# Position attention: the negated maxima become rows 96 to 98 of the query stack, moved there by DMA

## The reference

```
s[i, j]  = sum over 8 channels of q[i, .] * k[j, .]        i, j in 0..255   (k from ctx, q from x)
e[i, j]  = exp((s[i, j] - max over keys of s) * 8 ** -0.5)
o        = gamma * (v . e) / (sum of e) + x,   then layer norm over the 256 features
```

## Time and profile before

| | |
|---|---|
| median of 3 runs | 5330.28 us (5327.88 to 5330.65) |
| the profiled execution, its time | 5329.21 us |
| its span, first to last instruction | 5327.4 us |
| mean granted TensorE clock | 0.964 |
| PE, DVE, ACT, POOL busy | 88%, 63%, 40%, 30% of the span |

### The profile page before, as it was taken

How to read it: one execution, slowest core, us unless ns; L and a number is a source line. 1 busy time by engine, 2 the same in 40 slices (tenths; PEclk the granted TensorE clock), 3 DMA queues, 4 the chain that set the end, 5 groups by cost and what they waited for, 6 DMA issues and landing times.

```text
span 5327.4 us, 87975 instructions
## 1 busy us (share of the span) xinstructions
PE 4706.2 (88%) x32773; PEld 3287.9 (62%) x32773; DVE 3372.7 (63%) x6404; ACT 2108.9 (40%) x4198; POOL 1580.3 (30%) x3212
## 2 busy tenths in 40 slices
PE   8988985999979889883799999999987999999788
PEld 6766884666646677772466666666664556565455
DVE  5665245777767577787555555555545666666698
ACT  4543122545434333331344444444443343434222
POOL 1111015333312233432333333333332222222122
PEclk9999997999989999995899999999998999999899
DMA  1021002333310000001100000000001000000000
GB/s 41 2 61 46 1 6 62 73 76 76 74 48 1 5 8 8 8 7 65 44 1 1 1 1 1 1 1 1 1 1 36 5 6 5 5 6 4 3 15 16
DMA packets 106071, 109.35 MB, mean 21 GB/s; under 512 B 12144, under 2 KB 98353, under 8 KB 101169
## 3 DMA queue, kind: packets, MB, share of 16 engines
q1 hardware_dynamic: 105648, 103.72, 7.5%
HBM read 86.90 MB, written 16.78 MB: 19 GB/s over the span
## 4 chain that ended last, share of the span: by engine, by line
PE 47%; DVE 19%; issue 15%; POOL 10%; ACT 4%; DMA 3%; SPq 1%; POOLq 0%; DVEq 0%; ACTq 0%
PE banks L2207 12%; PE banks L2358 4%; POOL factors L2718 4%; PE banks L727 3%; PE banks L2343 2%; DMA stack<-parts_x 2%; PE banks L1172 2%; PE banks L2216 2%; PE banks L1761 2%; PE banks L754 2%; DVE neg_max L1085 1%; DVE stats L257 1%; PE banks L2226 1%; PE banks L1671 1%; PE banks L499 1%
## 5 line engine op out<-in xcount | busy, mean ns | idle before, releaser
L263 POOL TENSOR_TENSOR var_eps<-mean_var,ln_eps 128x1 f32<-128x1 f32 x384 | 83.6, 218 | 1633.3 <-DVE mean_var L259 1088.8
L1085 DVE TENSOR_REDUCE neg_max<-banks 128x2 f32<-128x512 f32 x512 | 343.6, 682 | 184.6 <-PE banks L1075 178.1
L1202 ACT ACTIVATE exps<-banks 128x512 f32<-128x512 f32 x512 | 304.8, 597 | 305.8 <-PE banks L1156 288.7
L2252 DVE TENSOR_REDUCE square_sums<-squares 128x4 f32<-128x512 f32 x256 | 174.7, 682 | 257.5 <-ACT squares L2244 253.5
L246 ACT COPY xT<-banks 128x256 f32<-128x256 f32 x160 | 59.7, 373 | 622.5 <-PE banks L238 359.2
L2265 POOL TENSOR_TENSOR factors<-mean_squares,minus_half 128x4 f32<-128x4 f32 x256 | 258.6, 1010 | 21.4
L2207 PE MATMUL banks<-wq,xT 128*128 128x512 f32 x512 | 245.8, 603 | 14.9 <-ACT xT L246 14.9
L1761 PEld LDWEIGHTS banks<-yT,w_swiglu 128*128 128x128 f32 x2048 | 238.2, 193 | 30.2 <-issue 30.0
L1075 PE MATMUL banks<-stack,stack 128*128 128x256 bf16 x1024 | 202.4, 281 | 60.7 <-DMA stack<-parts_x 55.2
L1761 PE MATMUL banks<-yT,w_swiglu 128*128 128x128 f32 x2048 | 247.4, 277 | 8.6 <-DVE hidden L1785 8.6
L2694 ACT ACTIVATE squares<-q_normed 128x512 f32<-128x512 f32 x160 | 100.8, 630 | 387.4 <-DVE q_normed L2684 387.4
(11 more groups left out here) (379 smaller groups left out, 11938.5 us busy)
## 6 DMA issues: line engine op xcount, KB each, us to landing
contextT<-in_ctxT SPq DMA_DIRECT2D x96, 128.0 KB, 3.1
parts_context<-parts SPq DMA_DIRECT2D x96, 64.0 KB, 2.0
parts_x<-parts SPq DMA_DIRECT2D x96, 64.0 KB, 2.0
stack<-parts_context SPq DMA_DIRECT2D x32, 192.0 KB
stack<-parts_x SPq DMA_DIRECT2D x32, 192.0 KB
x_all<-in_x SPq DMA_DIRECT2D x1, 4096.0 KB, 14.2
context<-in_ctx SPq DMA_DIRECT2D x64, 64.0 KB, 2.2
context<-in_ctx SPq DMA_DIRECT2D x32, 128.0 KB, 2.3
```

The lines of the kernel that those rows point to most:

```text
L1085: v.tensor_reduce(self.mx[s][:, :, g:g + 1], self.bM[g % 2].rearrange("p (h c) -> p h c", h=DH), AX.X, ALU.max, negate=True).then_inc(self ...
L1202: self.nc.scalar.activation(self.e[n % 8][:], self.bE[n % 2].rearrange("p (l c) -> p l c", l=DH), ACT.Exp, scale=self.TOK ** -0.5).then_in ...
```

## The change

- The scores no longer add the maxima with matmuls through `select` (L1156 and its table go). Instead SP moves the three rows of bf16 parts out of `neg_maxT` by three DMAs (`move_max_sp`) into rows 96, 97 and 98 of the query stack, and rows 96 to 127 of the key stack hold 1.0, set once by four more memsets on POOL. The score matmul then runs over all 128 rows, the maximum matmul over rows 0 to 95.
- `move_max_sp` stands first in SP's step, with lag 4, ahead of `stack_sp` with lag 2. The first score of a tile waits for the moves.
- The maxima are reduced two heads at a time (128 x 1024 from two banks, 8 instructions, odd ticks). The transposed maxima take one turn in the rotation of the two score banks, so the head scored next but one waits until ACT has copied them.
- Scores start at tick 10, not 6; a group is weighed in two halves two ticks apart; the last half of a tile stands at tick 13 of step t + 5, and `out_dve` and `tail_pool` run in step t + 6, the reciprocal in two halves.

```diff
-    STEP, SCORES_FROM = 16, 6
+    STEP, SCORES_FROM, TURN_AT = 16, 10, 4
+    ROWS, MAX_ROWS = 96, 128
+    TURN_SLOT = STEP - SCORES_FROM + TURN_AT
...
     def setup_pool(self, pool):
         for i in (0, 1):
             for n in range(self.STACK_BUFFERS):
-                pool.memset(self.kq[i][n][:].bitcast(I32), 0)
+                last = pool.memset(self.kq[i][n][:].bitcast(I32), 0)
+        last.then_inc(self.zeroed.sem, 1)
+        pool.wait_ge(self.zeroed.sem, self.zeroed.at(1))
+        for n in range(self.STACK_BUFFERS):
+            last = pool.memset(self.kq[0][n][self.ROWS:self.MAX_ROWS], 1.0)
+        last.then_inc(self.zeroed.sem, 1)
...
-            v.tensor_reduce(self.mx[s][:, :, g:g + 1], self.bM[g % 2].rearrange("p (h c) -> p h c", h=DH), AX.X, ALU.max, negate=True).then_inc(self.maxed.sem, 1)
+            v.tensor_reduce(self.mx[s][:, :, 2 * i:2 * i + 2].rearrange("p h g -> p g h"), self.bM[i % 2].rearrange("p g (h c) -> p g h c", h=DH),
+                            AX.X, ALU.max, negate=True).then_inc(self.maxed.sem, 1)
...
+    def slot_free(self, eng, slot):
+
+        t, n = divmod(slot - 2, self.HEADS + 1)
+        if slot < 2 or (n == self.TURN_SLOT and t + 1 >= self.NT):
+            return
+        if n == self.TURN_SLOT:
+            eng.wait_ge(self.m_copied.sem, self.m_copied.all(Tile(t + 1)))
+        else:
+            eng.wait_ge(self.exped.sem, self.exped.at(Tile(t), n + 1 - (1 if n > self.TURN_SLOT else 0)))
...
+    def move_max_sp(self, sp, t, s):
+
+        sp.wait_ge(self.m_copied.sem, self.m_copied.all(t))
+        for j in range(3):
+            sp.dma_start(self.stack(1, t)[self.ROWS + j:self.ROWS + j + 1, :, :],
+                         self.mT[s][32 * j:32 * j + self.HEADS, :]).then_inc(self.m_moved.sem(t), 16)
...
         for l in range(DH):
-            out = self.bE[n % 2][:, l * D:(l + 1) * D]
-            self.nc.tensor.matmul(out, k[:, h, l * P:(l + 1) * P], q[:, h, :], start=True, stop=False)
-            last = self.nc.tensor.matmul(out, self.sel[:, h, :], self.mT[s][:], start=False, stop=True)
+            last = self.nc.tensor.matmul(self.bE[self.slot(t, n) % 2][:, l * D:(l + 1) * D], k[rows, h, l * P:(l + 1) * P], q[rows, h, :], start=True, stop=True)
...
-            "pe": [[(5, self.score_late_pe), (4, self.score_pe), (4, self.turn_max_pe), (3, self.max_pe)]],
+            "pe": [[(6, self.weigh_last_pe), (5, self.score_late_pe), (4, self.score_from_pe), (4, self.turn_max_pe), (3, self.max_pe)]],
             "act": [[(5, self.exp_late_act), (4, self.exp_act), (4, self.copy_max_act)]],
-            "dve": [[(4, self.split_max_dve), (5, self.out_dve), (3, self.max_dve)]],
-            "pool": [(3, self.values_pool), (5, self.tail_pool), (1, self.split_pool)],
-            "sp": [(2, self.stack_sp), (1, self.parts_sp), (0, self.source_sp)],
+            "dve": [[(4, self.split_max_dve), (6, self.out_dve), (3, self.max_dve)]],
+            "pool": [(3, self.values_pool), (6, self.tail_pool), (1, self.split_pool)],
+            "sp": [(4, self.move_max_sp), (2, self.stack_sp), (1, self.parts_sp), (0, self.source_sp)],
```

More of the change, by code:

```diff
@@ L1117, in copy_max_act @@
     def copy_max_act(self, act, t, s):
-        for _ in range(4):
+        for _ in range(self.TURN_AT):
             yield
@@ L1121, in copy_max_act @@
         if begun(t - 2):
[L1122 to L1123 removed]
+            act.wait_ge(self.m_moved.sem(t - 2), self.m_moved.all(t - 2))
+        self.nc.scalar.copy(self.mT[s][:], self.bE[self.turn_slot(t) % 2].bitcast(BF16)[:, 0:D]).then_inc(self.m_copied.sem, 1)
+    def move_max_sp(self, sp, t, s):
[3 more added lines that the diff above has]
+                         self.mT[s][32 * j:32 * j + self.HEADS, :]).then_inc(self.m_moved.sem(t), 16)
     def values_pool(self, pool, t, s):
@@ L1165, in weigh @@
                 pe.wait_ge(self.o_read.sem, self.o_read.all(t - 2))
-        for part in range(4):
-            l, ones = divmod(part, 2)
+        for ones in (0, 1):
             for g in range(4):
@@ L1171, in weigh, with weigh_at, score_from_pe, score_late_pe @@
                 out = self.bO[s][32 * g:32 * g + 32, ones * D:(ones + 1) * D]
-                last = self.nc.tensor.matmul(out, left, self.e[n % 8][:, l, :], start=(r == 0 and part == 0),
+                last = self.nc.tensor.matmul(out, left, self.e[n % 8][:, l, :], start=(r == 0 and l == 0 and ones == 0),
                                              stop=(r == 3 and l == DH - 1), skip_group_check=True)
-        last.then_inc(self.weighed.sem, 1)
-    def score_pe(self, pe, t, s):
-        for tick in range(self.STEP):
-            if tick >= self.SCORES_FROM:
+        if l == DH - 1:
+            last.then_inc(self.weighed.sem, 1)
+    def weigh_at(self, pe, t, s, tick):
+        r, after = divmod(tick - self.SCORES_FROM - 5, 4)
+        if 0 <= r < 4 and after % 2 == 0:
+            self.weigh(pe, t, s, r, after // 2)
+    def score_pe(self, pe, t, s):
+        for tick in range(self.SCORES_FROM, self.STEP):
+            self.score(pe, t, s, tick - self.SCORES_FROM)
+            self.weigh_at(pe, t, s, tick)
+            yield
+    def score_from_pe(self, pe, t, s):
+        for _ in range(self.SCORES_FROM):
+            yield
+        yield from self.score_pe(pe, t, s)
+    def score_late_pe(self, pe, t, s):
+        for tick in range(self.STEP, 2 * self.STEP):
+            if tick - self.SCORES_FROM < self.HEADS:
                 self.score(pe, t, s, tick - self.SCORES_FROM)
-            for r in range(4):
-                if tick == self.SCORES_FROM + 4 * r + 5:
-                    self.weigh(pe, t, s, r)
+            self.weigh_at(pe, t, s, tick)
             yield
[L1185 to L1192, removed]
+    def weigh_last_pe(self, pe, t, s):
+        for tick in range(2 * self.STEP, 2 * self.STEP + 2):
+            self.weigh_at(pe, t, s, tick)
             yield
@@ L1218, in out_dve @@
         v = self.nc.vector
-        for _ in range(9):
+        yield
+        yield
+        dve.wait_ge(self.weighed.sem, self.weighed.all(t))
+        for half in (0, 1):
+            at = slice(half * P, (half + 1) * P)
+            v.reciprocal(self.rd[:, at], self.bO[s][:, D + half * P:D + (half + 1) * P]).then_inc(self.o_read.sem, 1)
             yield
-        dve.wait_ge(self.weighed.sem, self.weighed.all(t))
-        v.reciprocal(self.rd[:], self.bO[s][:, D:2 * D]).then_inc(self.o_read.sem, 1)
+            yield
+        dve.wait_ge(self.o_read.sem, self.o_read.at(t, 2))
+        v.scalar_tensor_tensor(self.on[s][:], self.bO[s][:, 0:D], self.gamma[:, 0:1], self.rd[:], ALU.mult, ALU.mult).then_inc(self.o_read.sem, 1)
         yield
-        dve.wait_ge(self.o_read.sem, self.o_read.at(t, 1))
-        v.scalar_tensor_tensor(self.on[s][:], self.bO[s][:, 0:D], self.gamma[:, 0:1], self.rd[:], ALU.mult, ALU.mult).then_inc(self.o_read.sem, 1)
         yield
```

63 lines of the change are left out of this document (36 added, 27 removed).

## The result

| | before | after |
|---|---|---|
| median | 5330.20 us (5327.88 to 5330.65, 4 runs) | 5407.51 us (5405.15 to 5419.81, 4 runs) |
| the profiled execution, its time and span | 5329.21, 5327.4 us | 5406.08, 5404.3 us |
| mean granted TensorE clock | 0.964 | 0.951 |
| PE, DVE, ACT, POOL busy | 88%, 63%, 40%, 30% | 86%, 62%, 39%, 29% |

The kernel became slower: 1.0151 times before, 95% interval 1.0133 to 1.0168. The forecast was 5399 us, in a range of 5338 to 5435.

What follows compares the result with a forecast made beforehand. Before, PE's work and a two-step loop through `mean_var`, POOL and the stack were taken to be in balance. Memsets 14.0, fill 2.0, 29 x (21.35 - 19.35) and drain -4.6 gave 69.4 us more: 5399 us, range 5338 to 5435.

Steps and rivals of the forecast that it cites:

- Loop of one step: From a PE step's first maximum matmul (S) through copy, moves and stack to PE's next start: 19.8 us.
- The falls: PE's idle lowers the clock in nine of ten steps, 1.7 us each: mean step 21.35 us.
- rival 1: The clock holds in PE's idles, so the step is 19.8 us and the kernel 5352 us; chance 0.22.
- 96 rows cost what 128 do: Maximum matmuls over 96 rows save PE nothing; at three quarters, 0.9 us of work would go.
- What I left off the path: Parts, DVE's work (some 15 us a step) and the moves' landing (0.9 us to spare) don't limit the step.
- two-step way: Through POOL, `mean_var` and the splits: parts land at S + 24.7 us, before SP comes to the stack at S + 26.9.
- Memsets: Four more memsets of ones on POOL, ahead of the first stack: 14.0 us by elements, 7.0 by bytes.
- Fill: Step 4, the first with a move ahead of a stack: 18.8 us in place of 16.8, +2.0.
- Drain: From tile 31's first maximum matmul to the last output's end: 44.0 us in place of 48.6, -4.6.
- The forecast's own range: 5360 to 5412 us, with moves at 1.2 to 1.95 us, memsets at 7 or 14, seven to ten falls in ten steps.
- Rival 2: The stack lands 2.5 us sooner, PE bounds a step of 16.6 us, the kernel takes 5259 us; chance 0.10.

Runs made afterwards that it cites:

- e4: The changed kernel with 22 matmuls of 256 columns that nobody reads ahead of each of PE's waits for a stack: 5357.80 us.
- e11: The changed kernel with POOL's splits first, the ones set by DVE, and the stack ahead of the moves on SP: 5265.47 us.
- e5: The changed kernel with the transpose of the maxima one tick earlier: 5384.36 us.
- e8: The changed kernel without the three moves and SP's wait for the copy, the maxima left out of the scores: 5345.73 us.
- e6: The changed kernel with the ones set by DVE beside POOL's zeros: 5389.69 us.
- e2: The changed kernel with the key stack's repeated blocks loaded one by one, nine DMAs in place of six: 5334.89 us.
- e7: The changed kernel with the key stack loaded by blocks, the transpose one tick earlier and the ones set by DVE: 5329.48 us.
- e1: The changed kernel with the moves issued by ACT behind its copy, the stack first on SP: 5431.82 us.

## Why the prediction was right

Each term as forecast, and what the traces show.

- **Loop of one step.** Forecast S to copy 5.1, wait and moves 1.95, stack to PE 12.77: 19.8 us. Measured in the chain above 5.05, 1.93 (1235.83 to 1237.76) and 12.78: 19.76. Taking the price of the moves from three stores in pieces of 512 B, not from stack loads, was right: SP needs 1.81 us for them.
- **The falls.** Forecast 0.9 x 1.7 us a step. The copy ended 6.4 to 8.0 us behind S in 25 of the 29 steps and 5.04 in four. Step 21.57 against 21.35, and e4 puts the falls at 1.67 us a step on average (48.4 us in all; forecast 44). That is fewer falls than forecast, but dearer ones: 48.4 over 25 is 1.94 us each, not 1.7. In 15 of them the copy came 1.3 to 1.6 us late, in the other ten 2.0 to 2.9. The Trainium skill's account ("TensorE: Matmul & The Clock Gate", section "HAM oscillation": a wait for a transfer in each tile throttles each tile) agrees in kind with these 25 of 29, though the waits of its example (about 3 to 5 us) are longer than most of those here. The prediction put the price of all 29 falling at 3 us over its sum; by its own terms it is 29 x 0.1 x 1.7 = 4.9.
- **But the argument for them was weaker than its result.** I expected idles of 3.6 us, beyond the 3.2 of the earlier trace rows, with PE's work at 16.2 us. e11 shows PE's work to be 16.99 us with nothing to wait for: 0.8 more. A half group takes 1.00 us in the chain above and the pair behind it 0.33 in place of 0.22, so 1.11 in all where I had 1.02, eight times a step. So the idles are about 2.6 us (2.2 to 3.8), near the 2.5 after which the clock held in the earlier trace rows. By that row I should have given rival 1 more than 0.22. The clock fell all the same, after 2.6 us here and after an idle of 1.8 us in e5 (at 1136.0 us), while it held after 2.8 us in the rows above and after 3.0 us at tile 6 (1036.5 us). That the falls came as forecast is thus in part luck: the length of idle they were argued from was not there, and no row of before shows an idle between 2.5 and 3.2 us.
- **96 rows cost what 128 do.** In the chain a pair of L1191 (128 rows) and a pair of L1088 (96 rows) take 0.22 us each.
- **What I left off the path.** Parts on the two-step way: forecast S + 24.7 us, in e8 1174.04 to 1198.93, 24.9. DVE: 158.7 us over 11.3 steps of e11, 14.0 a step, below PE's 17. The moves land before the first score: PE waited for them once in the section, 0.4 us.
- **Memsets.** Forecast 14.0, by elements: 13.87 for the four on POOL. On DVE (e6) each is recorded with 3.47 us too, but they start 4.27 us apart, with 0.80 us between them.
- **Fill.** Forecast +2.0 for the first step with a move: 929.99 to 948.81 us, 18.82 in place of 16.78. Tile 2 stands 15.25 us later than in the earlier trace rows, with the section beginning 0.7 us sooner.
- **Drain.** Forecast -4.6, measured 46.9 against 48.6 us: -1.7. Mis-sized by the same error in PE's half groups, in part; in e11, at full clock, it is 45.4 (1431.03 to 1476.47), where I had 42.3. The other 2 us were not taken apart.
- **Sum.** 15.25 + 29 x 2.22 - 1.7 = 78 us, against 76.9 between the profiled executions and 69.4 forecast. The forecast was 8 us low: 6.4 us in the step (0.22 x 29) and 2.9 in the drain, less 0.75 in the fill.
- **The forecast's own range.** 5360 to 5412 was not added up rightly at its upper end: with the loop at 19.8, ten falls in ten and memsets at 14, the terms give 16.0 + 29 x 2.15 - 4.6 = 74 us, 5403 us. The 5407.5 us measured are beyond that, since a fall cost 1.94 us and the drain gave 1.7 in place of 4.6.

Rival 2 (faster, 5259 us) was right in one thing: a step of about 17 us, PE bound, was to be had. The way to it is the order on SP and POOL, not a landing shortened by chance. Its counter-argument held in part: by the Trainium skill's "DMA: Bandwidth & Descriptors", section "Why a DMA increments its semaphore by 16 and not by 1", a repeated block of three runs on three engines and one of eight rows on eight. Loading by blocks did shorten issue to PE from 12.77 to 11.13 us, far less than that ratio of engines. In the tail 0.17 of sixteen engines were busy in the earlier trace rows, 2.7 on average, and 0.38, so 6.1, in e2, which agrees in kind. But no row names the engines, so what limits the rest of the landing stays open.

Open too is what decides a fall. Idles of 3.0 us with the clock held and of 1.8 us with a fall stand in traces of the same loop; the idle alone doesn't say. And why e8's steps alternate with falls at the ends of the section and not in its middle was not settled.

## What to carry to other kernels

- In a queue that runs in order, ask of each wait what stands behind it and in which step that is needed. A wait on this step's work ahead of a transfer for the next step closes a loop of one step; its length is the sum of latencies, whatever the busy shares say. Putting the early transfers and splits first, with the ones on DVE, gave 142 us together; what each would give alone was not measured, but for POOL's order (nothing) and the ones (18 us, 12 of them in the fill).
- A loop through PE pays the clock twice: an idle lets it fall, and the fall lengthens the loop. Price the loop at both levels.
- After shortening one loop look for the next (here POOL's, of two steps) before adding up small gains: e7's three edits gave 78 us together, where e2, e5 and e6 gave 114 added up.

## What the runs showed of the hardware

- Three rows of 8 KB, moved one by one between two places of the on-chip memory, land in 1.8 us each alone. Begun at about the start of a stack's load (96 rows of 8 KB), from 0.7 us ahead of it to 3.4 us behind, the last of them takes 7.0 to 8.8 us from another queue (e1), and 8.1 us from the same one 4 us behind (e11, in the fill). In the tail of that load, 8 to 10 us behind its start, they take 2.2 to 3.8 us (e11).
- Dummy matmuls in an idle of 2.6 us made the kernel 50 us faster (e4), since they kept the clock at 1.00.
- The clock fell after an idle of 1.8 us (e5) and held after one of 3.0 us (the changed kernel, tile 6).
- A memset of 4096 bf16 in a row takes 3.47 us on POOL (four in 13.87), twice one of 2048 int32 (eight in 14.03, 1.75 each), which sets as many bytes: there elements count. On DVE four of 4096 bf16 start 4.27 us apart.
